# Where the values matmuls stand in the last sixteen steps of an attention, with two PSUM banks for their results

## The reference

```
energy = einsum('nhqd,nhkd->nhqk', q, k)
attn = softmax(energy / sqrt(64), axis=3)
out = einsum('nhql,nhld->nhqd', attn, v)
out = out.reshape(N, -1, C) @ Wo.T + bo
x = x + out ;  t = t + ffn(ln(t))
```

## Time and profile before

| | us |
|---|---|
| median of 3 runs | 2573.31 (2571.03 to 2573.49) |
| profiled execution | 2568.86 |
| its span | 2567.1 |
| TensorE matmul busy | 2459.3 (96%) |
| DVE busy | 1945.7 (76%) |
| ACT busy | 1731.8 (67%) |
| POOL busy | 918.3 (36%) |

### The profile page before, as it was taken

One profiled execution on the slowest core, in us unless ns is written; L12 is line 12 of the kernel. 1 busy time (PEld: TensorE's weight loads), 2 busy tenths in 40 slices (PEclk: granted clock), 3 DMA queues, 4 the chain that ended last, 5 costly groups with the idle time before them and its releaser, 6 DMA issues.

```text
span 2567.1 us, 37185 instructions
## 1 busy us (share of the span) xinstructions
PE 2459.3 (96%) x13216; PEld 2015.1 (78%) x13216; DVE 1945.7 (76%) x3605; ACT 1731.8 (67%) x3083; POOL 918.3 (36%) x814
## 2 busy tenths in 40 slices
PE   7999999999999999999999999999999999999986
PEld 6788878887788777887878877788777887778874
DVE  5777777787777877778777787777867778677766
ACT  4777557774677746777377773777747776477754
POOL 2344414443144432443414433244422444234431
PEclk9999999999999999999999999999999999999998
DMA  7233213241223312324122340232402324023220
GB/s 276 62 83 116 86 31 93 75 132 66 66 67 79 123 63 66 78 66 136 50 77 68 79 141 33 78 87 60 155 17 84 81 70 144 30 86 79 59 77 33
DMA packets 80550, 215.14 MB, mean 84 GB/s; under 512 B 10384, under 2 KB 10608, under 8 KB 74608
## 3 DMA queue, kind: packets, MB, share of 16 engines
q1 hardware_dynamic: 80368, 212.77, 27.7%
HBM read 102.63 MB, written 25.17 MB: 50 GB/s over the span
## 4 chain that ended last, share of the span: by engine, by line
PE 77%; DVE 12%; ACT 7%; issue 2%; POOL 1%; DMA 1%; SPq 0%; ACTq 0%; DVEq 0%
PE pT L473 15%; PE pJ L439 10%; PE pO L488 9%; PE pO L489 9%; PE pS L460 7%; PE pS L461 7%; PE po L626 6%; PE pv L599 3%; ACT PR L706 2%; PE pv L439 2%; DVE PL L890 2%; ACT PH L740 2%; POOL PR L391 1%; PE pa L637 1%; DVE nmax L858 1%
## 5 line engine op out<-in xcount | busy, mean ns | idle before, releaser
L391 POOL TENSOR_SCALAR PR<-PR,rinv 128x1024 f32<-128x1024 f32 x512 | 577.6, 1128 | 1219.4 <-DVE rinv L862 1219.4
L740 ACT ACTIVATE PH<-pT 128x512 fp32r<-128x512 f32 x1024 | 558.7, 599 | 360.4 <-PE pT L473 347.1
L890 DVE TENSOR_TENSOR PL<-pT,PH 128x512 fp32r<-128x512 f32 x1024 | 657.6, 684 | 180.1 <-ACT PH L740 178.0
L858 DVE TENSOR_REDUCE nmax<-pS 128x1 f32<-128x1024 f32 x512 | 623.6, 1218 | 146.2 <-PE pS L461 145.3
L706 ACT ACTIVATE PR<-pS,nmax 128x1024 f32<-128x1024 f32 x512 | 576.3, 1126 | 4.2 <-DVE nmax L858 1.0
L473 PEld LDWEIGHTS pT<-ident,PR 128*128 128x128 f32 x4096 | 466.3, 141 | 128.9 <-POOL PR L391 47.8
L473 PE MATMUL pT<-ident,PR 128*128 128x128 f32 x4096 | 545.7, 275 | 21.7 <-DVE PL L890 15.4
L488 PE MATMUL pO<-PH,VS 128*128 128x512 f32 x1024 | 417.9, 408 | 6.4 <-DVE PL L890 6.4
L460 PE MATMUL pS<-KHL,QS 128*128 128x512 f32 x1024 | 411.4, 402 | 2.9 <-ACT PR L706 1.6
L489 PE MATMUL pO<-PL,VS 128*128 128x512 f32 x1024 | 404.0, 395 | 0.0
L461 PE MATMUL pS<-KHL,QS 128*128 128x512 f32 x1024 | 402.9, 393 | 0.0
(11 more groups left out here) (171 smaller groups left out, 3060.0 us busy)
## 6 DMA issues: line engine op xcount, KB each, us to landing
KHL<-HL SPq DMA_DIRECT2D x192, 256.0 KB, 3.4
X<-in_x SPq DMA_DIRECT2D x64, 512.0 KB, 6.5
WQ<-wqk_split SPq DMA_DIRECT2D x62, 512.0 KB, 4.3
QS<-HL SPq DMA_DIRECT2D x192, 128.0 KB, 3.0
WO<-wo_split SPq DMA_DIRECT2D x16, 1024.0 KB, 6.6
out<-X SPq DMA_DIRECT2D x16, 1024.0 KB, 4.7
KHL<-wv_split SPq DMA_DIRECT2D x14, 1024.0 KB, 8.5
KHL<-KHL SPq DMA_DIRECT2D x16, 512.0 KB, 4.3
```

The costliest lines, as they stand in the source:

```text
L391: pool.tensor_scalar(PR[g % 2][:, :], PR[g % 2][:, :], M["rinv"][:, g:g + 1], 1.0, ALU.mult, ALU.mult)\
L740: act.activation(PH[ck % 2][:, 4 * half:4 * half + 4, (g % 4) * P:(g % 4 + 1) * P], pT[half][:, :].rearrange("p (k n) -> p k n", k=4), ACT ...
L858: dve.tensor_reduce(nmax[:, g:g + 1], pS[g % 2][:, :], AX.X, ALU.max, negate=True).then_inc(S["a_max"], 1)
L890: dve.tensor_tensor(PL[ck % 2][:, ks, qs], pT[half][:, :].rearrange("p (k n) -> p k n", k=4), f32(PH[ck % 2][:, ks, qs]), ALU.subtract).th ...
```

## The change

In steps 49 to 63 TensorE's V stands behind T. All of steps 48 to 63 now have the order S T V. Each step still has four values matmuls. The finish of chunks 11 to 14 moves from g % 4 = 3 to the next step, g % 4 = 0: steps 52, 56, 60 and, for chunk 14, 64, which is a new item E64 at the head of ACT's and DVE's lists behind the attention. Since such a finish reads a bank in the step in which the next chunk's V begins to write, chunks 12 and 14 gather in pJ, and 11, 13 and 15 in pO. The waits follow: chunk 12 waits for the last copy out of pJ, chunks 13 to 15 for the addition of the chunk before the last one, and U0 waits for chunk 14.

```diff
-    "scalar": """H0 H1 H2 T0 T1 T2 T3 E67 ...
+    "scalar": """E64 H0 H1 H2 T0 T1 T2 T3 E67 ...
-    "vector": """H0 T0 T1 T2 T3 T4 E67 ...
+    "vector": """E64 H0 T0 T1 T2 T3 T4 E67 ...
...
+def out_bank(B, ck):
+
+    return B["pJ"] if ck in (12, 14) else B["pO"]
+
+
+def finished(g):
+
+    if g % 4 == 3 and (7 <= g < 48 or g > STEPS):
+        return g // 4 - 1
+    return g // 4 - 2 if g % 4 == 0 and 52 <= g <= STEPS else None
...
-            if ck >= 1:
-                wait("a_o", i, ck)
+            if ck == 12:
+                wait("a_proj_out", i, PER["a_proj_out"])
+            elif ck >= 1:
+                wait("a_o", i, ck - (ck > 12))
...
-            pe.matmul(pO[:, :], v, PH[ck % 2][:, kb, :], start=(kb == 0), stop=False)
+            pe.matmul(out_bank(B, ck)[:, :], v, PH[ck % 2][:, kb, :], start=(kb == 0), stop=False)
...
-        if 4 <= g < STEPS and g % 4 > 0:
+        if 4 <= g < 48 and g % 4 > 0:
             values(i, g // 4 - 1, 2 * (g % 4), 2 * (g % 4) + 2)
         elif STEPS < g < STEPS + 4:
             values(i, g // 4 - 1, *((0, 3), (3, 6), (6, 8))[g % 4 - 1])
         if 0 <= g < STEPS:
             turn(i, g)
-            if g >= 4 and g % 4 == 0:
-                values(i, g // 4 - 1, 0, 2)
+            if g >= 4 and g % 4 == 0 or g > 48:
+                values(i, g // 4 - 1, 2 * (g % 4), 2 * (g % 4) + 2)
...
-                wait(*(("a_proj_out", i, 12), ("a_o", i, 16))[n])
+                wait("a_o", i, 15 + n)
...
-        if g >= 7 and g % 4 == 3:
-            ck = g // 4 - 1
+        if finished(g) is not None:
+            ck = finished(g)
```

More of the change, by code:

```diff
@@ L219 @@
         A0 R0 R1 R2 R3 A1 R4 R5 A2 R6 R7 A3""",
[L220 to L225, removed]
+    "scalar": """E64 H0 H1 H2 T0 T1 T2 T3 E67 T4 T5 H3 T6 T7 N0 B0 B1 U0 U1 B2 U2 U3 U4 U5 U6 U7 V0 B3 S0 B4 B5 V1 V2 V3
+        V4 B6 B7 V5 F0 V6 F1 V7 L0 F2 F3 L1 L10 L2 L11 L20 Q0 Q1 L12 L21 L3 Q2 L13 L22 L23 A-1 Q3 A0 R0 R1 R2 R3
+        A1 R4 R5 A2 R6 R7 A3""",
+    "vector": """E64 H0 T0 T1 T2 T3 T4 E67 T5 H1 H2 O0 T6 T7 O1 O2 N0 O3 H3 O4 O5 O6 O7 B0 B1 U0 U1 U2 U3 U4 U5 B2 U6 U7
+        V0 S0 B3 S5 V1 S1 V2 B4 S2 B5 V3 V4 B6 B7 S3 V5 V6 L0 V7 L1 L10 L2 L11 Q0 Q1 L12 L3 Q2 L13 A-1 S4 D3 A0
+        A1 A2 A3""",
     "gpsimd": """H0 N0 S0 F0 A0 A1 A2 A3""",
@@ L230 @@
         Y10 L22 L13 R0 R1 R2 L23 R3 Y20 R4 R5 R6 R7""",
[L231 to L234, removed]
+    "scalar": """E64 H0 H1 E67 H2 H3 U0 U1 U2 U3 S10 U4 U5 U6 U7 F0 S20 F1 L0 L10 L1 F2 F3 L2 L20 L11 L3 L12 L21 L22 L13
+        R0 R1 R2 L23 R3 R4 R5 R6 R7""",
+    "vector": """E64 E67 H0 H1 O0 O1 O2 H2 H3 O3 O4 O5 O6 U0 U1 U2 U3 S10 O7 S15 S11 U4 S12 U5 S13 U6 U7 S20 S25 S21 S22
+        L0 S23 L10 L1 L2 L11 L3 L12 S14 L13 S24""",
     "gpsimd": """H0 S10 F0 F2""",
@@ L487, in values @@
             v = VS[:, kb, h, :]
-            pe.matmul(pO[:, :], v, PH[ck % 2][:, kb, :], start=(kb == 0), stop=False)
-            mm = pe.matmul(pO[:, :], v, PL[ck % 2][:, kb, :], start=False, stop=(kb == ST - 1))
+            pe.matmul(out_bank(B, ck)[:, :], v, PH[ck % 2][:, kb, :], start=(kb == 0), stop=False)
+            mm = pe.matmul(out_bank(B, ck)[:, :], v, PL[ck % 2][:, kb, :], start=False, stop=(kb == ST - 1))
         if last == ST:
@@ L719, in attend @@
                 wait("a_o", i, ck - 1)
-            act.activation(OB[ck % 2][:, :], pO[D:P, :], ACT.Identity,
+            act.activation(OB[ck % 2][:, :], out_bank(B, ck)[D:P, :], ACT.Identity,
                            bias=b_v[D:P, ck // 2:ck // 2 + 1]).then_inc(S["a_obot"], 1)
@@ L878, in attend @@
             dve.tensor_tensor(OT[n * D:(n + 1) * D, :, h * P:(h + 1) * P],
-                              pO[0:D, :].rearrange("d (j m) -> d j m", j=CT),
+                              out_bank(B, ck)[0:D, :].rearrange("d (j m) -> d j m", j=CT),
                               OB[ck % 2][:, :].rearrange("d (j m) -> d j m", j=CT), ALU.add).then_inc(S["a_o"], 1)
```

## The result

The changed kernel takes 2559.84 us (median of 5, 2556.67 to 2560.14) against 2571.03 of the kernel before (median of 5): ratio 0.9953, 95% interval 0.9938 to 0.9967, 11.2 us less. On a second chip session the same pair gave 2557.58 against 2572.29, ratio 0.9941 (0.9929 to 0.9954). The forecast was 2560.8.

A forecast was written before the change was run, and what follows sets the result against it. TensorE, holding 77% of the chain, was taken as the bound, with waits where the chain leaves it. 7 x 1.56 + 1.63 = 12.5 us off 2568.86 gives 2556.4; plus 4.45 for the median, 2560.8; range 2552 to 2569.

The forecast's parts named there:

- The waits between T's: From step 50 on: the change adds no instruction; what it costs or brings is in the waits, such as 1.00 before T(52).
- E65: TensorE's item behind T0 and T1 at the attention's end, waiting for the last low: forecast start 277.11, not 278.67.
- The norm chain takes over: End of S to next T: rowmax, recip and norm take 2.84 us against TensorE's step of 2.73; T's 2.86 to 3.00 apart.
- the walk: Step-by-step calculation of image 0 from T(50) to E65, each T starting at the latest of its limits.
- 1.56 us per image: E65 starts at 277.11 instead of 278.67; 1.63 in the last image, 12.5 us in all.
- The second bank and the finish: Chunk 12 need not wait for chunk 11's finish in step 52, and that finish finds V(51) ended long before.
- The edge covers E64: Behind the attention: E64's 0.7 us ACT copy before H0 stays hidden behind TensorE's work, with about 0.4 to spare.
- rival 2: Gain given back at the edge by E64's copy and addition or the residual's bias: 2566 to 2574; 16%, another rival included.
- Rival 1: Norm chain decides every step, slower: decides from 0.13 us per step, at 0.3 per step 16 us slower, 2590; 8%.
- Rival 3: More than forecast: norm follows closer, T(62)'s new wait is shorter; 2552, or 2545 with all steps' idle time gone; 14%.

The follow-up runs named there:

- the first swap: Changed kernel with DVE doing recip(g+1) before rowmax(g+2) from step 49 on: 2547.70 us, ratio 0.9912 to the kernel before.
- the second: Changed kernel with DVE doing recip(g+1) before rowmax(g+2) only from step 52 on: 2548.73 us, ratio 0.9913 to the kernel before.

## Why the prediction was right, point by point

- **The waits between T's are what the change is worth: right.** T(52) came at 243.08 once the late start is taken off (forecast 243.21), T(56) at 254.66 (254.81), T(62) at 271.90 (272.23), E65 at 276.89 (277.11).
- **The norm chain takes over: right in kind, a little too high in size.** Forecast 2.84 to 3.00 from T to T, measured 2.77 to 2.94, and 3.08 and 3.04 behind the finishes of steps 52 and 60. The chain from the end of S to T took 2.78 (238.57 to 241.35), where 2.84 was charged. So most T's come late by less than 0.1, which the list of waits does not show: it rose by 3.0 for the norm, and the forecast had some 10. Behind the finishes of 56 and 60 the walk took 2.86 where its own rule gives 2.90, 0.04 too little each. Where the norm arrived just before its T's turn, T took 0.84 (241.35 to 242.19) and not the 0.92 of a T behind a real wait, which I had charged. The swap of recip and rowmax shows the chain as cause: with it most steps take 2.74.
- **1.56 us per image: mis-sized.** It measured 1.77, in every image and in both traces of the changed kernel; the surplus of 0.2 is that of the late T's. 12.5 us became 14.1.
- **The second bank and the finish: right.** Without the bank the change loses 18 us, without the move of the finish 34. That the finish alone brings two thirds was not in the forecast, which did not split the gain.
- **The edge covers E64: right.** H0's copies ended and ACT's next two began at 281.04; TensorE's transposes wanted ACT at 282.41, for which ACT had waited 0.28 (the cover forecast at 0.4), and TensorE's only wait there is the 0.62 that was there before. But the edges gave back 2.9 us in this profile, by DVE and POOL taking turns. That is rival 2 in a part of its size, and by a mechanism that it did not name. In the second trace of the changed kernel it was 1.5.
- **Rival 1 (slower by the norm chain)** would need 0.13 more per step; the steps were shorter than forecast. Rival 3 was not reached by this change, but a small further edit got there.
- **The sum in time: close by luck.** In the terms of the profiled execution the forecast was 2556.4, 12.5 us less; it took 2559.84, 9.0 less. The attention gave 1.6 more than forecast, and the other stretches, put at nothing, gave back 5.1. That the median hits 2560.8 to 1 us comes from the 4.45 added for the distance of the median from the profiled execution: this time that distance was nothing.

What stays open: why the first swap and the second have the same time though the stretch differs by 0.23 us per image, 1.8 in all, less than the scatter of the two-valued stretches; and whether the change itself makes the long values more frequent. The traces have the long edge in four images of seven before, and in six and five of seven after. In most of them the start of POOL's second addition against OL's decides. Before, it lay from 0.15 us ahead of OL to 0.06 behind in six images of seven; in the first trace after, 0.01 to 0.12 ahead in all seven; but in the second again on both sides.

## What to carry to other kernels

Where one engine bounds a loop and the others are busy for most of it, look at what stands between two consecutive instructions of the chain that feeds it: three steps of one order and a fourth of another cost a wait at each seam, though each step alone is free. Where the matmuls that complete a bank stand last in their step, its evacuation belongs in the next step, and this needs a second bank: here one without the other lost 34 and 18 us. A change of 10 us in a run whose edges have two values each is read from one stretch of the trace, not from the total.

## What the runs showed of the hardware

- **Two-valued stretches by the clock.** The fourth row of the table, T(0) to T(48), differs by 0.9 to 1.4 us between images. Over the 13 traces and images 1 to 7, 33 of 34 longer values (167.5 us and up) have one time at the lower granted clock in them, and none of the 57 shorter ones has. In image 3 of the changed kernel the transposes behind two short idle times (1.18 and 0.89 us) run at half pace. The view by stretch (us, PE, PEld, DVE, ACT, POOL busy, PEclk, DMA share, GB/s), image 3 and then image 2 at the same work:

```profile
1003.60:1006.60 3.00, 2.93 (x13) 2.70 (x14) 2.58 (x5) 1.20 (x2) 1.12 (x1) 0.50 0.63 134
...
691.40:694.40 3.00, 2.67 (x18) 2.18 (x19) 2.59 (x5) 1.98 (x4) 1.12 (x1) 1.00 0.64 134
```

  The granted clock was 0.50, the level of 1.2 GHz, in one and 1.00 in the other; before it fell, TensorE had idled for the same 1.2 and 0.9 us in both. No run here shows why it falls in one image and not in the other. The tail's 1.4 us are partly the same: behind the last image's wait of 2.84 us four matmuls took 2.05 us before (clock 0.50) and 1.19 after (1.00).

```profile
2480.60:2483.20 2.60, 2.52 (x6) 2.07 (x7) 1.07 (x1) 0.00 (x0) 1.65 (x2) 0.50 1.00 386
```

- **DVE and POOL take turns** where DVE reads two operands from SBUF: 1.2 against 2.3 us for the same subtraction, about the length of one of POOL's additions (1.29 us alone) more. The one that starts first keeps its time, and the other one takes longer; where the starts lie within 0.03 us of each other, the traces show both outcomes.
